# Gate stage of a fused transformer kernel: exponential, marking and turning one step later in every engine's order, with three buffers of gates

## The reference

```python
z = jnp.einsum('nd,sdr->nsr', xf, P)
scores = jnp.einsum('nsr,smr->nsm', z, C)
topv, topi = jax.lax.top_k(scores, K)
w = jax.nn.softmax(topv, axis=-1)
```

## Time and profile before

| | us |
|---|---|
| Median of 3 runs | 1777.05 (1775.55 to 1780.81) |
| The profiled execution | 1783.77 |
| its span | 1782.1 |
| Gate stage in it | 886 to 1098.3 |

### The profile page before, as it was taken

How to read it: one execution, slowest core, us unless ns; L and a number is a source line. 1 busy time by engine, 2 the same in 40 slices (tenths; PEclk the granted TensorE clock), 3 DMA queues, 4 the chain that set the end, 5 groups by cost and what they waited for, 6 DMA issues and landing times. The chain is left out here.

```text
span 1782.1 us, 36039 instructions
## 1 busy us (share of the span) xinstructions
PE 1623.9 (91%) x13634; PEld 1114.5 (63%) x13634; DVE 985.6 (55%) x2733; ACT 738.0 (41%) x1416; POOL 572.9 (32%) x547
## 2 busy tenths in 40 slices
PE   7999789999996999979888887999999999889996
PEld 5677579976654899756555443222225775558886
DVE  2487732226858222268536756888886767932221
ACT  1266223324541111135424545999993553211110
POOL 1132121225411342365001213555552101325553
PEclk9999889999996999989998878999999999999998
DMA  6000445521005455202100116999991004026662
GB/s 230 1 2 2 162 162 186 185 92 30 20 2 205 160 182 181 69 25 103 36 21 20 44 51 224 398 389 366 355 335 38 1 2 158 1 79 188 194 189 32
DMA packets 97458, 228.12 MB, mean 128 GB/s; under 512 B 24297, under 2 KB 55753, under 8 KB 96393
## 3 DMA queue, kind: packets, MB, share of 16 engines
q1 hardware_dynamic: 77527, 206.03, 32.5%
q0 software_dynamic: 19552, 19.63, 4.5%
q10 hardware_dynamic: 210, 0.15, 0.0%
HBM read 198.81 MB, written 26.56 MB: 126 GB/s over the span
## 5 line engine op out<-in xcount | busy, mean ns | idle before, releaser
L2896 ACT ACTIVATE l2s_hidden<-ps,pack_l2f 128x816 f32<-128x816 f32 x256 | 227.1, 938 | 17.1 <-PE ps L2820 7.6
L2915 POOL TENSOR_TENSOR l2s_gated<-l2s_hidden,l2s_whole 128x408 f32<-128x408 f32 x128 | 136.0, 1063 | 103.0 <-PE ps L2828 103.0
L117 PE MATMUL ps<-pack_const 128*128 128x512 bf16 x574 | 147.8, 409 | 16.2 <-PEq L151 5.9
L2938 DVE TENSOR_TENSOR l2s_gated<-l2s_hidden,l2s_whole 128x816 f32<-128x816 f32 x128 | 142.7, 1115 | 28.7 <-ACT l2s_hidden L2896 26.1
L2395 POOL DMA_INDIRECT l_xt<-rows_in,l_tokens x66 | 63.0, 954 | 244.4 <-PE ps L2408 186.9
L2436 PE MATMUL ps<-l_down,l_hidden 128*128 x792 | 139.8, 326 | 0.0
L2436 PEld LDWEIGHTS ps<-l_down,l_hidden 128*128 128x128 f32 x792 | 127.3, 190 | 0.4
L117 PEld LDWEIGHTS ps<-pack_const 128*128 128x128 bf16 x574 | 57.1, 104 | 88.1 <-issue 38.5
L2419 PE MATMUL ps<-l_xtT,l_up 128*128 128x128 f32 x792 | 99.4, 275 | 3.4 <-DVE l_xtT L2671 3.4
L2419 PEld LDWEIGHTS ps<-l_xtT,l_up 128*128 128x128 f32 x792 | 96.7, 192 | 4.3 <-DVE l_xtT L2671 4.3
L2515 ACT ACTIVATE l_hidden<-ps,l_down 128x128 f32<-128x128 f32 x198 | 54.8, 376 | 89.9 <-PE ps L2424 89.9
(11 more groups left out here) (548 smaller groups left out, 3580.8 us busy)
## 6 DMA issues: line engine op xcount, KB each, us to landing
l2s_whole<-g_whole SPq DMA_DIRECT2D x128, 612.0 KB, 7.1
l_up<-in_l_up SPq DMA_DIRECT2D x66, 576.0 KB, 3.8
l3c_wg<-in_l_gate SPq DMA_DIRECT2D x16, 576.0 KB, 4.9
l3c_wu<-in_l_up SPq DMA_DIRECT2D x16, 576.0 KB, 6.4
l3c_wd<-in_l_down SPq DMA_DIRECT2D x16, 576.0 KB, 3.8
slots_out<-l_y SPq DMA_DIRECT2D x66, 96.0 KB, 2.3
l_down<-in_l_down SPq DMA_DIRECT2D x8, 675.0 KB, 9.0
l_down<-in_l_down SPq DMA_DIRECT2D x8, 576.0 KB, 7.2
```

The costliest lines, as they stand in the source:

```text
L117: pe.matmul(bank, halves[:, 0:128], halves[:, :], start=True, stop=True)
L2896: act.activation(hidden[:, p % kept, :, :], ps[:, 0, 2 * (p % 2):2 * (p % 2) + 2, 0:NG], ACT.Gelu_apprx_tanh, bias=w.at("b1")[:, s * MT + ...
L2915: pool.tensor_tensor(gated[:, (4 * n + 1) % ring, :], hidden[:, 2 * n % kept, 1, :], whole[:, n % ahead, 0, :], ALU.mult).then_inc(late_re ...
L2938: dve.tensor_tensor(gated[:, at:at + 2, :], hidden[:, (2 * n + 1) % kept, :, :], whole[:, n % ahead, 1:3, :], ALU.mult).then_inc(gated_rea ...
```

## The change

The exponential, the multiplication and the turning of a sample come one step later: GpSimd subtracts sample t-1 in step t as before, ScalarE takes the exponential of t-2 (now ahead of the score copy), VectorE multiplies t-2 (now ahead of the markings of t-1), TensorE turns t-3, and ScalarE, VectorE and GpSimd treat the turned gates of t-3. Bias and share products come one step later too: t % 4 == 3 and 1. The differences, the exponentials and the gates of a sample lie in one buffer of three, in place, and `expo` is gone. There is one step more.

```diff
-        marked, expo = spare["x"].take(L, NS, NM + KEEP), spare["x"].take(L, NS, NM)
-        chosen = spare["x"].take(L, 2, NS, NM)
+        marked = spare["x"].take(L, NS, NM + KEEP)
+        chosen = [spare["x"].take(L, NS, NM) for _ in range(3)]
...
-        LAST = B + 5
+        LAST = B + 6
...
-            for t in range(B + 2):
-                c, e = t // GB, t - 2
+            for t in range(B + 3):
+                c, e = t // GB, t - 3
...
-                    if n:
-                        pool.wait_ge(chosen_ready, n)
-                    pool.tensor_tensor(expo[:, :, :], score[:, n % 2, :, 0:NM], kept[:, n, :, 0:1].broadcast_to([L, NS, NM]),
+                    if n >= 3:
+                        pool.wait_ge(gT_ps, n - 2)
+                    pool.tensor_tensor(chosen[n % 3][:, :, :], score[:, n % 2, :, 0:NM], kept[:, n, :, 0:1].broadcast_to([L, NS, NM]),
                                        ALU.subtract).then_inc(below_ready, 1)
...
-                biased, shared = (t - 6) // GB if t % GB == 2 else -1, (t - 8) // GB if t % GB == 0 else -1
+                biased, shared = (t - 7) // GB if t % GB == 3 else -1, (t - 9) // GB if t % GB == 1 else -1
...
-                n = t - 2
+                n = t - 3
                 if 0 <= n < B:
                     pe.wait_ge(chosen_ready, n + 1)
...
-                                            chosen[:, n % 2, 2 * r:2 * r + 2, :].rearrange("p s m -> p (s m)"),
+                                            chosen[n % 3][:, 2 * r:2 * r + 2, :].rearrange("p s m -> p (s m)"),
...
-                biased, shared = (t - 6) // GB if t % GB == 2 else -1, (t - 8) // GB if t % GB == 0 else -1
+                biased, shared = (t - 7) // GB if t % GB == 3 else -1, (t - 9) // GB if t % GB == 1 else -1
                 if 0 <= t < B:
                     act.wait_ge(zT_ps, t + 1)
                     act.activation(zT[:, :, :].rearrange("p c n -> p (c n)"), zT_bank, ACT.Copy).then_inc(zT_ready, 1)
+                n = t - 2
+                if 0 <= n < B:
+                    act.wait_ge(below_ready, n + 1)
+                    act.activation(chosen[n % 3][:, :, :], chosen[n % 3][:, :, :], ACT.Exp).then_inc(expo_ready, 1)
...
-                if 0 <= t - 1 < B:
-                    act.wait_ge(below_ready, t)
-                    act.activation(expo[:, :, :], expo[:, :, :], ACT.Exp).then_inc(expo_ready, 1)
-                n = t - 2
+                n = t - 3
...
+                past = t - 2
+                if 0 <= past < B:
+                    steps.wait()
+                    dve.wait_ge(expo_ready, past + 1)
+                    dve.scalar_tensor_tensor(chosen[past % 3][:, :, :], marked[:, :, 0:NM], MARK, chosen[past % 3][:, :, :],
+                                             ALU.is_ge, ALU.mult).then_inc(chosen_ready, 1)
                 if 0 <= n < B:
                     dve.wait_ge(best_ready, n + 1)
...
-                if 0 <= n < B:
-                    steps.wait()
-                    dve.wait_ge(expo_ready, n + 1)
-                    if n >= 2:
-                        dve.wait_ge(gT_ps, n - 1)
-                    dve.scalar_tensor_tensor(chosen[:, n % 2, :, :], marked[:, :, 0:NM], MARK, expo[:, :, :],
-                                             ALU.is_ge, ALU.mult).then_inc(chosen_ready, 1)
-                e = t - 2
+                e = t - 3
```

## The result

| | us |
|---|---|
| Before, median of 5 runs | 1777.05 (1774.13 to 1780.81) |
| After, median of 5 runs | 1791.76 (1789.73 to 1797.34) |
| After / before | 1.0084, 95% interval 1.0061 to 1.0107 |
| Profiled execution after | 1789.73, its span 1788.0, clock 0.949 |

The change makes the kernel 14.7 us slower. I had forecast 1775.4, the range ended at 1784.0, and even the rival on the slower side said 1782.9. The mechanism of that rival came true, and at about its price: it said 7.5 us, and the runs put it at 7.7 to 9.2. The rest of the miss lies in my walk through the steps, above all in step 7 and in the tail.

What follows compares the result with a forecast made beforehand. No engine was taken as full in the gate stage; what counted was where TensorE waits. The terms -1.8 + 2.5 - 4.0 + 0.8 + 0.9 = -1.6 us, on 1777.05, gave 1775.4 us; range 1768.5 to 1784.

Steps and rivals of the forecast that it cites:

- the rival on the slower side: GpSimd's subtraction, starting first, delays VectorE's multiplication 0.89 us a step: 7.5 us in all, 1782.9 us; chance 0.25.
- my walk through the steps: The gate stage's 22 steps in order, asking what TensorE waits for: -1.6 us, error 3 to 4 us, chance 0.45.
- the hold: VectorE's multiplication held behind GpSimd's subtraction, both reading two SBUF tensors; priced at 7.5 us, only in a rival.
- Step 3: The copy for the projection comes earlier, so the projection directly follows the score matmul: -1.8 us.
- Steps 4 to 6: ScalarE stops waiting for GpSimd but waits as long for VectorE's difference of the turned gates: no gain.
- Step 7: Bias products move here, before the out products: 3.3 us, of which VectorE hides 0.8, so +2.5 us.
- Step 8: Share products leave this step, so the mix transposes follow projection and turning sooner: -4.0 us.
- Steps 9 to 11: Shares ahead of the gate products cost 1.4 us, bias products move from 10 to 11: +0.8 us together.
- Tail: Steps 12 and later: 2.2 us of score-copy waits return, exponentials ahead cost 2.1, the added fill 1.0: +0.9 us.
- I cost this reordering at nothing: VectorE's multiplication moved ahead of the eight markings: zero, with -0.2 and +0.9 us per step as ends.
- Rival 3: Gaps in step 7 drop TensorE to its lower clock, out products take 4.2 us: +3 to 4 us, 1779; chance 0.12.
- Rival 2: Bias chain in steps 7 and 11 and the tail's additions are hidden: -5.8 us, 1771.3 us; chance 0.18.

Runs made afterwards that it cites:

- e11: The changed kernel, unchanged, run again for a second profile: 1.01 of the kernel before, gate stage 219.6 us.
- e1: The changed kernel with one added wait: GpSimd's subtraction starts only after VectorE has finished the multiplication of its step; 1.0032 of the kernel before.
- e7: The kernel before with only bias and share products one step later, and the step added at the end: 1.0032 of the kernel before.
- e8: The changed kernel with the multiplication at the head of VectorE's step, ahead of the eight largest: 0.9997 of the kernel before.
- e4: The kernel before, unchanged, run again for a second profile: 0.9977, profiled execution 1776.00 us, gate stage 206.8 us.
- e10: The changed kernel with multiplication first in VectorE's step, bias products at t % 4 == 0, and scores and first-share copy moved ahead in the tail: 0.9968.

## Why the prediction was wrong, point by point

**The account.** The change costs 14.9 us by its first measurement, 17.8 by the second (e11). Taking away the hold alone (e1) leaves 5.7, so the hold is worth 9.2 us by the ratios and 7.7 by the profiles. The 5.7 that are left are what the moved chains cost alone (e7, with an interval from 0.4 to 10.8). e8 then gains 6.2 us on e1. I put that down to the multiplication standing in VectorE's idle time; the intervals of the two overlap, and no run has that alone.

The terms of my sum against the profiles, each from z of one step to z of another, less the same stretch in e4:

| | Forecast | The change | e1 (nothing held) |
|---|---|---|---|
| Step 3 (start to z of step 4) | -1.8 | -4.5 | -4.5 |
| Steps 4 to 6 | 0 | +1.8 | +0.2 |
| Step 7 | +2.5 | +6.5 | +5.2 |
| Step 8, to the mix transposes | -4.0 | -2.8 | -2.4 |
| Mix transposes to z of step 9 | 0 | 0.0 | +4.4 (at half clock) |
| Steps 9 to 11 | +0.8 | +2.2 | +0.9 |
| Tail (z of step 12 to the end) | +0.9 | +9.7 | +5.8 |
| Sum | -1.6 | +12.8 | +9.5 |

**"I cost this reordering at nothing."** This is the first step that failed: 7.7 to 9.2 us where I had nothing. The argument was the order within VectorE alone: the same instructions, the same drain. That much was right (2.68 us before and 2.67 in e1). What changed was who else works at that moment. The markings that stood there before were not held: in e4 one at 1056.71, inside GpSimd's subtraction from 1055.78 to 1056.84, takes 0.21 us like the others. The rival named it, with place and delay right: I had 0.89 us of delay and it is 0.88 (1.575 of the median against 0.69). Its chance, 0.25, hung on who comes first. I had rows for both answers: the start of GpSimd 0.03 us ahead of VectorE's next instruction, and the pair at 431, where VectorE ran unhindered though recorded 0.10 us later. The first was of the very place, the second of another stage and other shapes, and I let the second weigh as much. In the change GpSimd was first in 14 of 16.

The Trainium skill, SBUF — State Buffer, section "SBUF: two separate sides", has the pair of ports held by the one that starts first until its instruction ends. The steps of the kernel after agree, both ways: 1.58 us with GpSimd 0.03 ahead, 0.69 with VectorE 0.17 ahead. By that rule the forecast would have been my rival's 1782.9, on the right side and still 9 us short.

**The walk.** This is the second step that failed. With nothing held I had -1.6 us, and e1 measured +5.7 by its ratio and +5.1 by its profile without the 4.4 us at half clock. What was too low or too favourable is step 7, step 8 and the tail, by 2.7, 1.6 and 4.9 us; step 3 gave 2.7 us more than I took.

**The price of the hold.** I counted eight steps at 0.89 us and 0.4 at the end, 7.5 in all, which is close to the 7.7 of the profiles. The places are less well hit. Steps 4 to 6 lose 1.6 us by it (the change less e1), where I had counted 2.7; step 7 loses 1.3, where I had counted none; the tail loses 3.9, where I had counted 3.1 (three steps of 0.89, and 0.4). A held multiplication also delays the difference behind it, then ScalarE's second part, then the bias or share products at the head of TensorE's queue (2.45 and 2.34 us).

**Step 3, -1.8: right in kind, too small.** The projection follows the score matmul directly, and the out products come 2.6 us sooner; at the turning of z in step 4 it is 4.5. TensorE's granted clock is 0.90 over the 4.8 us from 960.9 in the change, and 0.50 over 4.8 us from 963.6 in e4, where a gap of 1.93 us stands ahead of the projection. Two lines of e4, then two of the change, from TensorE's timelines:

```profile
965.04 0.97 PE L1760 MATMUL ps<-pack_l2a,pack_l0f 64*102 64x192 f32 x4
965.94 1.60 PE L1757 MATMUL ps<-pack_l2a,pack_l0f 128*102 128x192 f32 x4
```

```profile
962.15 0.57 PE L1760 MATMUL ps<-pack_l2a,pack_l0f 64*102 64x192 f32 x4
962.65 0.90 PE L1757 MATMUL ps<-pack_l2a,pack_l0f 128*102 128x192 f32 x4
```

**Steps 4 to 6, nothing.** ScalarE waits for the difference of the gates instead, as I wrote; with the hold this is a loss of 1.8 us, without it (e1) of 0.2.

**Step 7, +2.5.** The bias products stand before the out products, as forecast. I had reckoned 3.3 us for them, from z of step 7 to the out products. With nothing held it is 3.7 (e7) and 4.4 (e1), with the hold 5.4 (9.1 us against 3.7). Rival 3 had part of the rest. The first out products take 1.49 us and all sixteen 4.4, where it said 4.2. But the change's clock had fallen before the gaps of step 7: it was 1.00 up to 999 us, 0.60 from 999 to 1001 and 0.50 from 1001 to 1013, after pauses of 1.58 and 0.74 us around the fused transposes; in e1 it fell within step 7 (0.69 from 1001 to 1003, then 0.50). And group 4 did not begin lower, since the change's mix ran at 1.00. The 0.8 us that I let VectorE hide doesn't appear: z of step 8 is another 1.1 us later.

**Step 8, -4.0.** Right in kind: the mix transposes follow the turning. But the 5.7 us of the earlier trace rows were at half clock, in the execution of the higher kind. From the turning of z to the mix transposes it is 4.6 us in e4 and 1.8 in the change: -2.8.

**Steps 9 to 11, +0.8.** z of step 9 to z of step 12: 25.9 us in e4, 28.1 in the change, +2.2, inside my bounds for it (-0.7 to +2.5).

**The tail, +0.9.** It is +9.7, the largest miss, and the hold is 3.9 of it. With nothing held it is still +5.8 (e1). It is +2.1 only in e8, where VectorE's step is shorter and the granted clock is 0.92, against 0.82 in e4. What I didn't do was to follow the chains into steps 13 and 15 and ask what their products wait for, though I had asked it for steps 7 and 9; and I didn't see that the copy of the first shares now stands behind the last exponential. That wait is 2.10 us in the change and 2.49 in e1.

**Rival 2** (gains alone, 1771.3) did not come true. e10 reached 1771.3 us, but only with bias and share products moved to other places. **The size of the reference.** I noted that the profiled execution stood 6.7 us above its median and assigned that to no place; between z of steps 8 and 9 it had lost 7.2 us to e4, 3.2 of them in the very stretch from which I read the term of step 8. **The chances.** The parts that I named for the two outer results add up to some 0.14 and 0.17, not 0.18 and 0.20.

What stays open: why at 431 VectorE ran unhindered though recorded later than GpSimd (the change's profile repeats it: 432.75 and 432.84, GpSimd 1.39 us where the next one of its kind takes 0.59); why step 7 and the tail cost more than reckoned beyond the waits named here; and what decides whether the mix of group 4 runs at the upper or the lower level in a kernel that hasn't changed. No run was made for either.

## What to carry to other kernels

Before moving an instruction within one engine's queue, look at what the other engines do at its new moment, VectorE and GpSimd above all: coming second cost the multiplication 0.37 to 0.88 us here, fourteen times, and some of the delays were passed on to what waits for the end of the step. Look for a place for it that lies ahead of the instruction that releases the other engine, best where its own engine is waiting anyway (e8). And when products move to another step, ask in every such step what they wait for, up to the last. And read a term from a second profile when the first is well above its median: the excess sits in one place, which may be the one that you read.

## What the runs showed of the hardware

- VectorE's multiplication (102x512 f32, both inputs in SBUF) beside GpSimd's subtraction of the same size: 1.57 us if GpSimd is recorded 0.03 first, 1.42 at 0.18 first, 1.06 at 0.54 first, 0.69 if VectorE is 0.17 first. Whenever it was held it ended 0.54 to 0.55 us after GpSimd's end. GpSimd's subtraction took 1.43 in place of 1.06 when it was second, and its small third part of z 0.81 in place of 0.36 when it fell into the held multiplication. VectorE's markings (102x68) beside the same subtraction kept their 0.21 us.
- The same TensorE work in the same kernel, without a gap, was granted 0.50 in one execution and 1.00 in another: 8 us from the mix transposes on, which took 11.6 us up to z of step 9 in the one and 7.7 in the other.
